# A decoder layer on one core: another order of full-array work between the score pairs of the attention loop

## The reference, cut to what matters

```python
x = layernorm(x + self_attention(x))                      # rotated queries and keys
x = layernorm(x + cross_attention(x, ctx, mask) @ Wo.T + bo)
x = layernorm(x + moe(x))                                 # 8 experts, top 2, capacity, exact gelu
# attention, per batch and head:
scores = q @ k.T / 4
out = softmax(scores) @ v
```

## Time and profile before

| | us |
|---|---|
| median of 3 runs | 2501.18 |
| lowest, highest | 2500.62, 2502.72 |
| profiled execution, its own time | 2499.03 |
| its span | 2497.3 |
| TensorE busy in the span | 2220.8 (89%) |
| VectorE busy | 1249.2 (50%) |
| ScalarE busy | 974.0 (39%) |
| GpSimd busy | 586.3 (23%) |

### The profile page before, as it was taken

How to read it: one execution, slowest core, us unless ns; L and a number is a source line. 1 busy time by engine, 2 the same in 40 slices (tenths; PEclk the granted TensorE clock), 3 DMA queues, 4 the chain that set the end, 5 groups by cost and what they waited for, 6 DMA issues and landing times. The chain is left out here.

```text
span 2497.3 us, 52990 instructions
## 1 busy us (share of the span) xinstructions
PE 2220.8 (89%) x18752; PEld 1533.9 (61%) x18752; DVE 1249.2 (50%) x2596; ACT 974.0 (39%) x1474; POOL 586.3 (23%) x910
## 2 busy tenths in 40 slices
PE   5899999999999999999999999988399999999940
PEld 3566666666666666666666666655277777777730
DVE  3366666666666666666666666653111111111116
ACT  0254555455554555445545555542122122122100
POOL 0012222322223222232223222221112122122122
PEclk7799999999999999999999999987599999999975
DMA  8001100010001000000000000000223233133126
GB/s 247 9 15 31 35 30 26 30 40 26 22 23 33 30 26 20 23 29 24 19 21 24 29 23 19 24 21 11 67 66 76 71 79 67 26 73 78 15 55 231
DMA packets 111837, 113.43 MB, mean 45 GB/s; under 512 B 12096, under 2 KB 107405, under 8 KB 111776
## 3 DMA queue, kind: packets, MB, share of 16 engines
q1 hardware_dynamic: 85792, 85.87, 11.2%
q0 software_dynamic: 17664, 18.35, 4.3%
q10 hardware_dynamic: 8320, 8.39, 1.0%
HBM read 64.53 MB, written 56.05 MB: 48 GB/s over the span
## 5 line engine op out<-in xcount | busy, mean ns | idle before, releaser
L835 DVE TENSOR_REDUCE smax<-ps_s 128x4 f32<-128x1024 f32 x512 | 625.7, 1222 | 458.1 <-PE ps_s L555 430.6
L718 ACT ACTIVATE prob<-ps_e 128x1024 f32<-128x1024 f32 x512 | 524.0, 1024 | 654.1 <-PE ps_e L564 593.1
L555 PE MATMUL ps_s<-stack 17*128 17x256 f32 x4096 | 593.1, 407 | 74.8 <-ACT stack L706 45.8
L564 PE MATMUL ps_e<-stack 18*128 18x256 f32 x4096 | 594.9, 409 | 11.9 <-ACT prob L718 11.6
L555 PEld LDWEIGHTS ps_s<-stack 17*128 17x128 f32 x4096 | 359.8, 188 | 287.4 <-issue 185.7
L564 PEld LDWEIGHTS ps_e<-stack 18*128 18x128 f32 x4096 | 358.2, 188 | 27.8 <-ACT prob L718 15.6
L580 PE MATMUL ps_w<-prob,val 128*32 128x256 f32 x4096 | 302.6, 446 | 25.4 <-DVE val L847 25.4
L1403 ACT ACTIVATE hid<-m_ps_h,b_sb 128x320 f32<-128x320 f32 x256 | 134.9, 527 | 431.5 <-PE m_ps_h L1365 431.5
L1365 PE MATMUL m_ps_h<-m_cols,w_sb 128*128 128x320 f32 x1024 | 280.3, 435 | 0.6 <-DVE m_cols L1415 0.6
L1379 PE MATMUL m_ps_o<-w_sb,hid 128*128 128x256 f32 x1280 | 279.1, 379 | 0.6 <-ACT hid L1403 0.6
L1379 PEld LDWEIGHTS m_ps_o<-w_sb,hid 128*128 128x128 f32 x1280 | 242.2, 190 | 33.1 <-ACT hid L1403 1.1
(11 more groups left out here) (120 smaller groups left out, 2178.7 us busy)
## 6 DMA issues: line engine op xcount, KB each, us to landing
w_sb<-in_w SPq DMA_DIRECT2D x16, 1024.0 KB, 7.6
slot_rows_dram<-fill SPq DMA_DIRECT2D x8, 1290.0 KB, 14.5
m_rows<-slot_rows_dram SPq DMA_DIRECT2D x16, 645.0 KB, 7.2
xT<-in_xT SPq DMA_DIRECT2D x32, 256.0 KB, 2.6
ctxT<-in_ctxT SPq DMA_DIRECT2D x32, 256.0 KB, 2.6
x_res<-in_x SPq DMA_DIRECT2D x32, 256.0 KB, 2.7
stack<-nrows SPq DMA_DIRECT2D x512, 2.0 KB
sums_dram<-x SPq DMA_DIRECT2D x32, 256.0 KB, 2.2
```

Source lines behind the costliest of these rows:

```text
L555: mm = nc.tensor.matmul(ps_s[:, s_bank(X, p), t, :], stack[X][rows, Q, p // HG, t * P:(t + 1) * P], stack[X][rows, K, p // HG, :], start=T ...
L564: mm = nc.tensor.matmul(ps_e[:, p % 2, t, :], stack[Y][rows, K, h // HG, t * P:(t + 1) * P], stack[Y][rows, Q, h // HG, :], start=True, st ...
L718: nc.scalar.activation(prob[:, h:h + 2, :].rearrange("p h s -> p (h s)"), ps_e[:, :, :, :].rearrange("p h t s -> p (h t s)"), ACT.Exp, sca ...
L835: nc.vector.tensor_reduce(max_columns(X, p), ps_s[:, :, :, :], AX.X, ALU.max)\
```

## The change: what it does

The hardware loop and all instructions stay. In the table `at`, SELF's values move from behind pair 2 to behind pair 7, its projections from 3 and 6 to 2, 3 and 5 (the first in two parts), x2's transposes from 5 to 3, the x1 columns from 5 to 4, the key stack and the routing product from 7 to 6. CROSS's values stand wholly behind pair 7, its key stack behind 5 and its query stack behind 6. ScalarE's copies to send move from m = 6 to m = 5. On VectorE the normalisation of x2 moves from the end of CROSS to behind the first maximum of the SELF slot that follows, both value copies stand right behind the last maximum of their slot, and the second `cross_part` comes one pair earlier.

```diff
--- before.py
+++ after.py
@@ -296,10 +296,10 @@
 
 
 
-        at = [dict(out_rows=1, values=(2, 2), project=(3, 3, 6, 6), columns=5, x2_columns=5,
-                   stack_k=7, stack_q=7, route=7),
-              dict(out_rows=1, project=(2, 2, 3, 3), columns=5, count=5, values=(5, 7), project_out=6,
-                   stack_k=7, stack_q=7)]
+        at = [dict(out_rows=1, project=(2, 3, 5, 5), x2_columns=3, columns=4, stack_k=6, route=6,
+                   stack_q=7, values=(7, 7)),
+              dict(out_rows=1, project=(2, 2, 3, 3), columns=5, count=5, stack_k=5, project_out=6,
+                   stack_q=6, values=(7, 7))]
         MAX1, STACK_K1, STACK_Q1, MAX0 = 1, 1, 2, 5
 
 
@@ -784,7 +784,7 @@
                         columns(X, bX - 1)
                     if there(bX) and m == MAX0:
                         max_rows(X, bX, 0)
-                    if there(i - 3) and X == SELF and m == 6:
+                    if there(i - 3) and X == SELF and m == 5:
                         rows_to_send(i - 3)
                     if there(i - 3) and X == CROSS and m == 1:
                         gates(i - 3)
@@ -1015,6 +1015,8 @@
                     if there(bX) and p % 2 == 0:
                         maxima(X, bX, p)
                     if X == SELF:
+                        if there(i - 3) and p == 1:
+                            second_normed(i - 3)
                         if there(bX - 1) and p == 3:
                             divide(SELF, bX - 1, 0)
                             divide(SELF, bX - 1, 1)
@@ -1022,12 +1024,12 @@
                             first_norm(bX - 1)
                         if there(bX - 1) and p == 7:
                             first_normed(bX - 1)
-                        if there(bX) and p == 7:
-                            values(SELF, bX)
                         if there(bY + 1) and p == 9:
                             cross_part(bY + 1, 0)
-                        if there(bY + 1) and p == 13:
+                        if there(bY + 1) and p == 11:
                             cross_part(bY + 1, 1)
+                        if there(bX) and p == 15:
+                            values(SELF, bX)
                     else:
                         if there(i - 3) and p == 1:
                             routing_logits(i - 3)
@@ -1045,12 +1047,10 @@
                             positions(i - 3)
                         if there(bX - 1) and p == 13:
                             second_norm(bX - 1)
-                        if there(bX - 1) and p == 15:
-                            second_normed(bX - 1)
+                        if there(bX) and p == 15:
+                            values(CROSS, bX)
                         if there(i - 3) and p == 15:
                             own_positions(i - 3)
-                        if there(bX) and p == 15:
-                            values(CROSS, bX)
 
             turn(0, 0)
             turn(0, 1)
```

## The result

The changed kernel takes **2399.96 us** (median of 4 runs, 2397.67 to 2403.8), the kernel before 2501.28 in the same set (2500.62 to 2502.72). The ratio is 0.9596 (95% interval 0.9579 to 0.9612): 4.0% faster, 101 us. The forecast was 2414, so the gain is 14 us larger, and the measurement lies 0.04 under the lower edge of the range (2400 to 2440). The profiled execution took 2399.15, with a span of 2397.4 and a mean clock of 0.946 (0.924 before).

What follows compares the result with a forecast made beforehand. TensorE's queue bounds the loop: 51.20 us per iteration less waits gave 46.94, with new losses about 48.2, a gain of 3.0; 28 x 3.0 + 2.7 = 87 off 2499.0 gave 2412, median 2414; range 2400 to 2440.

Steps and rivals of the forecast that it cites:

- The bound: In the attention loop TensorE's own queue sets the time: busy 48.6 of 51.20 us per iteration.
- The clock term, 1.62: Behind the back edge, beat 0's product runs at half clock, 3.55 us instead of 1.94; 1.62 per iteration goes.
- (a): Rival: one low-clock stretch per iteration survives elsewhere, price 1.65 us; 49.9 per iteration, time 2460; chance 0.11.
- (c): Rival: thin beats SELF 3 and CROSS 5 bring two low-clock stretches at 1.65 us each; time 2509; chance 0.06.
- the thin place: Stretch around the loop's back edge: each iteration pays about 1.75 us of TensorE waits and 1.62 of low clock.
- The value-copy wait, 0.82: In beat 0, the product's wait for VectorE's late value copy goes: 0.82 us per iteration.
- (b): Rival: beat 0's product still waits and the clock still falls; iteration stays 51.2 us, time 2500; chance 0.05.
- The back edge, 0.93, against a fetch: The 0.93 us idle at the loop's jump is priced by the last release; if it stays in full, time 2427.
- New VectorE waits: Norm work on VectorE delays maxima: 0.49 us lost in SELF beat 3 and 0.45 in CROSS beat 7.
- The floor of 2.60: Between one score pair's start and the next, in any beat: at least 2.60 us because of VectorE's maximum.
- The normalisation of x2 at 1.57: Moved behind SELF's first maximum on VectorE: takes 1.57 us, free with 0.1 to spare; at worst 0.8 per iteration.
- The ends, 0 within 5 each way: Partly filled iterations at both ends: moved filler may gain or lose there, bounded by 5 us each way.

Runs made afterwards that it cites:

- e4_again: Kernel before with only the SELF row of the table and its order on VectorE and ScalarE changed, in a quiet set: 2463.97 us, ratio 0.9841.
- e2b_filled_gap: Kernel before with four unused multiplications of constants added in TensorE's idle gap at CROSS's end, value copy left in place: 2451.77 us, ratio 0.9805.
- e1_again: Kernel before with only CROSS's value copy put ahead of the normalisation of x2 on VectorE, in a quiet set: 2417.25 us, ratio 0.9667.
- e1_copy_first: Kernel before with only CROSS's value copy put ahead of the normalisation of x2 on VectorE, in a disturbed set: 2489.09 us, ratio 0.9928.
- e6_later_moments: Changed kernel with the moments of both norms one maximum later on VectorE: 2392.94 us, ratio 0.9557, in a quiet set; 2495.12, 0.9946, in a disturbed one.

## Why the prediction was right, and where a term was off

- **The bound** (TensorE's queue, and only what fills or idles it): right. The counted work, 46.94, and the gaps above it gave 48.1 beat by beat; measured 48.09, SELF 23.95 for 23.8, CROSS 24.14 for 24.3.
- **The clock term, 1.62**: right in size, and shown alone by e4_again (51.12 to 49.49, 1.63, with every wait the same); in e2b_filled_gap it is 1.61 beside the wait of 0.73. Rivals (a) and (c), a low stretch elsewhere or two, didn't come: SELF 3 and CROSS 5 ran at 1.00. That the thin place was made of two waits is borne out too: no run that lost one of them, quiet or disturbed, had a low stretch at the back edge in iterations 4 to 31, with the 0.93 left in place in e1_again and e1_copy_first. In e4_again the gaps of 0.93 and 0.75 come with a fall eight times and then without one to the end of the loop. The Trainium skill, "TensorE: Matmul & The Clock Gate", Why this matters for your kernels, names gaps over about 3 us as what to avoid; here shorter ones could bring the fall, and their length alone didn't decide it.
- **A reading that was wrong**: rival (a) said that the clock fell at 1656.5 where no long wait stood. TensorE waited 0.80 for a maximum there, no less than the 0.75 at the back edge, in the timeline of the kernel before:

```profile
1655.21 0.49 PE L555 MATMUL ps_s<-stack 17*128 17x256 f32 x2 [0.80 <-DVE smax L835]
```

So that fall speaks less for (a) and (c) than the prediction took it to. The price of (c), 2509, is also 3 us above 28 times its 3.3 on 2414.
- **The value-copy wait, 0.82** of beat 0: right. S0 is 2.94 and no wait for the copy is left, so rival (b) falls.
- **The back edge, 0.93, against a fetch**: right. The edge is taken at every pass and shows 0.21 idle (forecast 0.4); C7 is 3.28 (forecast 3.35). The next pair comes 0.54 behind the end of the last maximum (forecast 0.68 behind the last release). In e1_again the 0.94 stands at the same edge with the old releaser, and in e6_later_moments and e2b_filled_gap no idle time stands there at all. The rule of the Trainium skill, "Runtime: NRT & Kernel Launch", Instruction fetch mechanics, would have left it in full, had the jump gone outside what was fetched; the loop shows no such cost. The page of the profile counts 40 and 21 packets of instructions for the whole program, and in the trace none of them starts between 277.2 and 1535.6 us of after, or between 286.3 and 1628.3 of before: most passes fetched nothing.
- **New VectorE waits**: they stand where the sum put them. SELF 3 waits 0.54 and is 3.13 (forecast 0.49 and 3.03); CROSS 7 is 0.38 over its work of 2.90 (forecast 0.45). Taking the moments out of the way gave 0.44 and 0.27 of that back in e6_later_moments, and lost 0.24 in SELF 4.
- **The floor of 2.60** was 0.07 too high in CROSS 5: that beat is 2.53, and no wait is recorded before the pair that ends it (1043.01). Over the loop that is 2 us.
- **The normalisation of x2 at 1.57**: mis-sized. It takes 0.73 in its new place (1004.13). In the earlier trace rows one of its two instructions took 1.25 and the other 0.40; beside the long one stood GpSimd's addition of the output bias, which has no such neighbour now:

```profile
1005.54 1.26 POOL L1109 TENSOR_TENSOR x1b<-x,bias_o 128x512 f32<-128x512 f32 x1
```

The 14 traces agree, from 186 to 1620 us: where the two overlap, by 0.48 to 1.21 us, the instruction takes 0.63 to 1.35, in all 289 cases 0.15 more than the overlap; where they don't, it takes 0.39 to 0.46. The conclusion, free, holds with more to spare.
- **The ends, 0 within 5 each way**: the term that failed. They gave 10.3. The prediction took them as filler that may win or lose; the 5.4 of iteration 32 came from the clock instead, and the other 4.9 were not traced to a cause. In iteration 32 the low stretches fell from 34.1 us to 23.9, and they stand in other places of the slots. e1_again, with the old table, ran iteration 32 in 48.53 instead of 58.84, 13.7 of it at low clock instead of 34.1, which the table can't have done. With e6_later_moments the same term had the other sign. So this part of the gain is luck, as far as the prediction goes. The full iterations were 3.6 better than the 87 of the sum (3.11 for 3.0, and 3.9 in the first). So of the 14 us between forecast and result 10.3 are the ends, twice their bound, and they put the median 0.04 under the range.

## What to carry to other kernels

Price a low-clock stretch by the row of the same work at full clock (here 3.55 against 1.94), and look for it behind the thinnest place of the busiest engine. Removing one of the two waits there gave 2.43 us per iteration, filling the place with useless work still 1.61. Count the falls over the whole loop before pricing the next change: the same order can run with them and without (e4_again). Where a stage is partly filled at its ends, bound its time by all its work at either clock, not by the filler moved there. Measure a reordering in more than one set of runs: this one is 4% faster in two sets and 1.5% slower in a third, where a version with fewer waits behind VectorE (e6_later_moments) was still 0.5% faster than the kernel before.

## What the runs showed of the hardware that was not expected

- **One order of work, two clocks.** e4_again ran its first iterations at 51.05 to 51.37 with a fall in each, and the others at 49.49 with none, the waits being equal.
- **TensorE finishing late.** The same kernels took 2417 and 2489, 2415 and 2546, 2464 and 2556, 2395 and 2547, 2393 and 2495, in a quiet set and in a disturbed one; the kernel before has medians of 2500 to 2509 in all sets, though with single runs from 2494 to 2540 in the disturbed ones. The difference lies in SELF's beats 1 to 4, where a pair's semaphore comes up to 3.35 us behind its last multiplication instead of 0.40, while GpSimd issues four indirect transfers (1064.58 to 1069.52 in e1_copy_first). In the quiet sets those transfers stand beside the same beats (1005.05 to 1010.0 in after) and nothing is late. The first set bears the same chip's number (10) as the two quiet ones, the fourth another (3), so it isn't the chip alone, as far as that number tells chips apart.
- **What stays open.** Whether these transfers cause the lateness wasn't tried (no run moved them), nor why the kernel before keeps its time; it was not profiled in a disturbed set. Its mean granted clock there is 0.928 to 0.945, most often 0.94, instead of 0.922 to 0.925 in the quiet ones. As an estimate from 0.942 and 0.924 over 2500 us, that is 90 us less at half clock, as much as 26 of its stretches of 3.41 us. So it seems to lose time there as well and to get it back by having lost its low stretches; without a trace this isn't shown, nor is the argument that its S1 and S2 come 2.4 us later, behind the long product.
